# A DLRM tower on one core: products from split halves against fp32 products in row strips, and sixteen looked-up fields against twelve

## What is computed

```python
e = jnp.stack([tbl_0[ids[:, 0]], ..., tbl_38[ids[:, 38]]], axis=1)    # (512, 39, 32), fp32
p, q = e[:, ROW, :], e[:, COL, :]                                     # all 741 pairs i < j
z = jnp.einsum('bpc,apc,bpa->bp', p, w, q)                            # w: (32, 741, 32)
h = jnp.concatenate([z, dense_ctx], axis=1)                           # 741 + 16 = 757
h = jnp.maximum(h @ W_top1 + b_top1, 0.0)                             # 512
h = jnp.maximum(h @ W_top2 + b_top2, 0.0)                             # 256
y = h @ W_top3                                                        # (512, 1)
```

## Time and profile before

| | |
|---|---|
| median of 3 runs | 220.56 us (220.49 to 225.24) |
| span of the profiled execution | 285.0 us |
| PE, DVE, ACT, POOL busy in it | 198.8, 146.6, 97.5, 134.8 us |
| moved by DMA | 31.40 MB |

### The profile page before, as it was taken

One profiled execution on the slowest core, in us unless ns is written; L12 is line 12 of the kernel. 1 busy time (PEld: TensorE's weight loads), 2 busy tenths in 40 slices (PEclk: granted clock), 3 DMA queues, 4 the chain that ended last, 5 costly groups with the idle time before them and its releaser, 6 DMA issues.

```text
span 285.0 us, 2687 instructions
## 1 busy us (share of the span) xinstructions
PE 198.8 (70%) x974; PEld 73.5 (26%) x974; DVE 146.6 (51%) x115; ACT 97.5 (34%) x142; POOL 134.8 (47%) x134
## 2 busy tenths in 40 slices
PE   0048668453212277738798197699899999999996
PEld 0012223000000033213333032243333334344341
DVE  0353794101000027824794266389599779898230
ACT  2516899300000047830540071037127127110032
POOL 7774767777777300776587887200042015007000
PEclk9999797755555559795999669599999999999999
DMA  4869779700000003997266018148715846450000
GB/s 134 257 210 300 285 177 212 164 16 13 14 13 13 9 0 74 300 207 148 50 158 166 12 41 183 41 96 167 167 33 118 183 98 129 98 121 1 0 2 0
DMA packets 11352, 31.40 MB, mean 110 GB/s; under 512 B 3230, under 2 KB 7098, under 8 KB 10379
## 3 DMA queue, kind: packets, MB, share of 16 engines
q1 hardware_dynamic: 7882, 29.45, 42.1%
q0 software_dynamic: 3456, 1.78, 3.5%
HBM read 12.34 MB, written 0.00 MB: 43 GB/s over the span
## 4 chain that ended last, share of the span: by engine, by line
PE 51%; issue 18%; DMA 9%; DVE 7%; SPq 6%; another core or an unknown queue 4%; ACT 3%; DVEq 0%; ACTq 0%
PE t_ps L719 16%; PE z_ps L735 15%; PE z_ps L688 9%; DMA mlp<-tbl 6%; PE side_ps L750 5%; DMA wring<-w_lo 4%; DVE prod L658 3%; SPq L425 2%; PE t_ps L777 2%; DVE prod L629 2%; SPq L431 1%; SPq L475 1%; PE t_ps L765 1%; PE t_ps L770 1%
## 5 line engine op out<-in xcount | busy, mean ns | idle before, releaser
L658 DVE TENSOR_TENSOR prod<-t_ps,eT 128x1536 f32<-128x1536 f32 (+2 forms) x70 | 109.9, 1600 | 79.3 <-PE t_ps L719 49.7
L514 POOL DMA_INDIRECT gathered<-tbl,ids_sb x108 | 104.9, 971 | 53.5 <-issue 31.4
L719 PE MATMUL t_ps<-stack,wring 128*128 128x512 f32 x210 | 72.9, 464 | 12.2 <-issue 6.7
L735 PE MATMUL z_ps<-prod,sel 128*32 128x512 f32 x380 | 57.5, 645 | 4.6 <-issue 4.6
L719 PEld LDWEIGHTS t_ps<-stack,wring 128*128 128x128 f32 x210 | 38.3, 205 | 65.8 <-issue 39.5
L688 PE MATMUL z_ps<-prod,room 125*32 125x512 bf16 x72 | 21.0, 534 | 34.1 <-issue 33.3
L528 POOL TENSOR_TENSOR room<-room,w_hi 128x512 f32<-128x512 f32 x3 | 3.9, 1286 | 66.3 <-ACT w_hi L603 66.3
L629 DVE TENSOR_SCALAR prod<-mlp,slice_rows 125x2048 bf16<-125x2048 f16 x18 | 14.8, 856 | 23.0 <-remote 23.0
L587 ACT ACTIVATE stack<-hi_lo 32x512 fp32r<-32x512 f32 x39 | 24.6, 629 | 2.6 <-issue 1.2
L580 ACT ACTIVATE stack<-eT 32x512 fp32r<-32x512 f32 x39 | 24.4, 625 | 1.0 <-PE t_ps L719 0.7
L750 PE MATMUL side_ps<-room,mlp 128*128 128x512 f32 x32 | 18.4, 660 | 7.7 <-ACT eT L567 7.6
(11 more groups left out here) (49 smaller groups left out, 113.5 us busy)
## 6 DMA issues: line engine op xcount, KB each, us to landing
wring<-w_hi SPq DMA_DIRECT2D x30, 224.0 KB
wring<-w_lo SPq DMA_DIRECT2D x30, 224.0 KB
stack<-stack SPq DMA_DIRECT2D x9, 512.0 KB
w_lo<-wst SPq DMA_DIRECT2D x4, 896.0 KB, 15.2
eT<-hot_ids SPq DMA_DIRECT2D x3, 1024.0 KB
gathered<-tbl,ids_sb POOLq DMA_INDIRECT x108
mlp<-w SPq DMA_DIRECT2D x1, 1536.0 KB
mlp<-tbl SPq DMA_DIRECT2D x12, 125.0 KB
```

What stands on the lines that cost most here:

```text
L514: pool.indirect_dma_start(gathered[:, n % GATHER_BUFS, b, K * r:K * r + K], None, tables[f], bass.IndirectOffsetOnAxis(ap=ids_sb[:, F * b ...
L658: dve.tensor_tensor(prod[:, g % XSLOTS, 0:n, :], t_ps[g % 2][:, 0:n, :], field, ALU.mult).then_inc(multiplied, 1)
L719: mm = pe.matmul(t_ps[g % 2][:, i, :], wring[:, c % WSLOTS, passes % WCHUNK, :].bitcast(F32R), stack[:, J % STACKS, src - G * J, :].bitcas ...
L735: mm = pe.matmul(z_ps[K * (u % G):K * (u % G) + K, :], sel[:, u // G, :], prod[:, g % XSLOTS, t - TILE_BASE[g], :], start=(u < G), stop=(u ...
```

## The change

It rewrites the kernel in these parts:

- **Products.** No halves, no stack, no ring. All weights (55 tiles of 128 columns) are loaded once and used in fp32. A "quad" is block J against block I: its four tiles use the four strips of 32 rows of `eT[:, J, :]` and of the same weight tile, so each product has 32 rows and 128 columns. A block against itself is two products of 64 rows (one of 96 for the last block). DVE multiplies two tiles at a time; three such pairs fit in PSUM, where two groups of three did.
- **Lookups.** Four blocks (0, 1, 2 and 4: 16 fields) instead of three. The upper 16 bits of the table words are used where they lie, as bf16; the two lower bytes become two bf16 parts (two ACT instructions for each block), and the results are put together in `eT` as two 16-bit halves. PE spreads the ids over the partitions itself. The fourth block has ten slices.
- **Gathers.** Six blocks (23 fields, 92 gathers), each with its own buffer. After each gather but the last POOL clears an unused tile of 128 x 256 and waits for the clear before it.
- **Tower.** Early sums in three rounds of 2, 2 and 1 blocks of z; nothing is left of the fifth block for the end.
- All plain loads are issued at the start.

```diff
-HOT_BLOCKS = [0, 1, 3]
-GATHERED = [J for J in range(NBLK) if J not in HOT_BLOCKS]
+LOOKED = [0, 1, 2, 4]
+GATHERED = [J for J in range(NBLK) if J not in LOOKED]
+SMALL = [f for f in range(F) if TABLE_ROWS[f] == 1000] + [f for f in range(F) if TABLE_ROWS[f] == 1250]
+HOT_FIELDS = [SMALL[G * h:G * h + G] for h in range(NHOT)]
+NSLICE = [TABLE_ROWS[fields[0]] // HP for fields in HOT_FIELDS]
...
+for _J in range(NBLK):
+    QUADS += [(_J, _I, FIELDS_IN[_J]) for _I in range(_J)]
+    QUADS.append((_J, _J, 2 if FIELDS_IN[_J] == G else 1))
...
+PAIRS = [(q, i, min(2, QUADS[q][2] - i)) for q in range(NQUAD) for i in range(0, QUADS[q][2], 2)]
+TSLOTS = 3
+XSLOTS = 6
-ROUNDS = [[0], [1], [2], [3]]
+ROUNDS = [[0, 1], [2, 3], [4]]
+KEEP_LEAD = 3
...
+    steps += [("ids", 0), ("lower", 0), ("ids", 1), ("look", 0, 0, 3), ("lower", 1), ("ids", 2), ("look", 0, 3, 8),
+              ("keep", 0), ("lower", 2), ("ids", 3), ("look", 1, 0, 8), ("lower", 3), ("keep", 1), ("look", 2, 0, 8),
+              ("keep", 2), ("quad", 0), ("look", 3, 0, 2), ("quad", 1), ("look", 3, 2, 5), ("quad", 2),
+              ("look", 3, 5, 8), ("quad", 3), ("look", 3, 8, 10), ("keep", 4), ("keep", 3)]
+    sums(1, True)
+    for q in range(4, NQUAD):
+        steps.append(("quad", q))
+        for T in GATHERED[1:]:
+            if q == FIRST_QUAD[T] - KEEP_LEAD:
+                steps.append(("keep", T))
...
-                for i, part in enumerate((w_hi, w_hi, w_lo, w_lo)):
-                    sp.dma_start(wring[K * i:K * i + K, c % WSLOTS, :, :].rearrange("p a b -> p (a b)"),
-                                 part[q:q + K, c // G, :]).then_inc(wring_in[c % WSLOTS], 16)
+            def load_w(J):
+                a, b = W_BASE[J], W_BASE[J + 1]
+                sp.dma_start(w_sb[:, a:b, :].rearrange("p t c -> p (t c)"),
+                             wst[:, P * a:P * b]).then_inc(w_in[J], 16)
...
+                    pool.indirect_dma_start(
+                        gathered[J][:, b, K * r:K * r + K], None, tables[f],
+                        bass.IndirectOffsetOnAxis(ap=ids_sb[:, F * b + f:F * b + f + 1], axis=0),
+                    ).then_inc(rows_in[J], 16)
+                    if pauses:
+                        pool.wait_ge(paused, pauses)
+                    if (J, r, b) != (*fields[-1], NCHUNK - 1):
+                        pool.memset(pause[:, :], 0.0).then_inc(paused, 1)
+                        pauses += 1
...
+                        act.activation(lower[i][h][0:HP, :, :], bytes_of[h][0:HP, :, 1 - i::4], ACT.Copy,
+                                       scale=256.0 if i == 0 else 1.0).then_inc(lower_made, 1)
...
+                        act.activation(words.bitcast(BF16)[:, 1::2], look_ps[h][0], ACT.Copy)
+                        act.activation(words.bitcast(U16)[:, 0::2], look_ps[h][1], ACT.Copy).then_inc(eT_made, 1)
...
+                        dve.tensor_tensor(prod[:, p % XSLOTS, 0:n, :], ps[:, s:s + n, :],
+                                          eT[:, I:I + 1, :].broadcast_to([P, n, B]), ALU.mult).then_inc(multiplied, 1)
...
+                    for r in range(G):
+                        mm = pe.matmul(ids_ps[h][:, r, :], spread[:, G * h + r, :], ids16[:, :], start=True, stop=True)
...
-                            mm = pe.matmul(t_ps[g % 2][:, i, :],
-                                           wring[:, c % WSLOTS, passes % WCHUNK, :].bitcast(F32R),
-                                           stack[:, J % STACKS, src - G * J, :].bitcast(F32R),
-                                           start=(k == 0), stop=(k == len(tile) - 1))
+                        if p >= TSLOTS:
+                            pe.wait_ge(multiplied, p - TSLOTS + 1)
+                        for i in range(first, first + n):
+                            rows = source_rows(q, i)
+                            mm = pe.matmul(ps[:, 2 * (p % TSLOTS) + i - first, :], w_sb[rows, w_tile(q), :],
+                                           eT[rows, J, :], start=True, stop=True)
+                        mm.then_inc(t_made, 1)
```

More of the change, by code:

```diff
@@ L77 @@
+FIRST_TILE = [TILE_BASE[q] + i for q, i, _ in PAIRS]
+PAIRS_THROUGH = [sum(1 for p in PAIRS if p[0] <= q) for q in range(NQUAD)]
+TSLOTS = 3
+XSLOTS = 6
 ZTILES = P // G
 ZM = ZTILES // G
[L81 to L109, removed]
@@ L126, with sources @@
-FIRST_GROUP = [min(g for g in range(NGROUP) if GROUPS[g][0] == J) for J in range(NBLK)]
-ROUNDS = [[0], [1], [2], [3]]
[L128 to L133, removed]
-SEL_LAG = 2
+NZ = -(-NTILE // ZTILES)
+ROUNDS = [[0, 1], [2, 3], [4]]
+SEL_LAG = 2
+KEEP_LEAD = 3
+PACE = 2
+Z_LAG = 2
+PAUSE = 256
+def sources(q):
+    J, I, n = QUADS[q]
+    if I < J:
+        return [[(r, c) for c in range(G)] for r in range(n)]
+    if FIELDS_IN[J] == G:
+        return DIAGONAL
+    return [LAST_DIAGONAL]
@@ L137, in plan @@
+_free = [z_row(t, c) for t in range(NTILE) for c in range(G) if (t, c) not in _taken]
+DENSE_ROWS = []
+while len(DENSE_ROWS) < NDENSE // 2:
+    _a, _b = _free[:2]
+    if _a // P == _b // P:
+        DENSE_ROWS.append((min(_a, _b), abs(_a - _b)))
+    _free = _free[2 if _a // P == _b // P else 1:]
+DENSE_BLOCKS = sorted({first // P for first, _ in DENSE_ROWS})
 def plan():
     steps, done = [], 0
[L155 removed]
@@ L156, in plan @@
[L156 to L161, removed]
+    early = [(m, n) for n in range(len(ROUNDS)) for m in range(M1)]
+    since = 0
     def sums(upto, exact):
@@ L205, in plan, with there @@
-    sums(NGROUP - 2, True)
-    steps += [("early", *e) for e in early]
-    steps += [("long", k) for k in range(long, NZ - 1)]
-    late = [("late", m, zb) for m in range(M1 - 1) for zb in range(EARLY_Z, NZ - 1)]
-    steps += late[:-1]
-    sums(NGROUP - 1, True)
-    steps += late[-1:]
-    return [step for step in steps if step not in POOL_WORK.values()]
+    def there(zb):
+        names = [s[:2] for s in steps]
+        return ("z", zb) in names and sum(s[0] == "quad" for s in names[names.index(("z", zb)):]) > Z_LAG
@@ new lines, in plan @@
+    steps += [("ids", 0), ("lower", 0), ("ids", 1), ("look", 0, 0, 3), ("lower", 1), ("ids", 2), ("look", 0, 3, 8),
[4 more added lines that the diff above has]
+    for q in range(4, NQUAD):
+        J = QUADS[q][0]
+        steps.append(("quad", q))
+        since += 1
+        for T in GATHERED[1:]:
+            if q == FIRST_QUAD[T] - KEEP_LEAD:
+                steps.append(("keep", T))
+        near = any(0 < FIRST_QUAD[T] - KEEP_LEAD - q <= 1 for T in GATHERED)
+        if early and since >= PACE and not near and all(there(zb) for zb in ROUNDS[early[0][1]]):
+            steps.append(("early", *early.pop(0)))
+            since = 0
+        sums(q - SEL_LAG, False)
+        sums(q - SEL_LAG - 1, True)
@@ L215 @@
+    sums(NQUAD - 2, True)
+    steps += [("early", *e) for e in early]
+    sums(NQUAD - 1, True)
+    return steps
 PLAN = plan()
-LAST_FIRST = [M1 - 1] + list(range(M1 - 1))
-assert NGROUP % 2 == 0
-SPLITS = [s[1:] for s in PLAN if s[0] == "split"]
 TURNS = [s[1] for s in PLAN if s[0] == "keep"]
-assert all([s[1] for s in PLAN if s[0] == part] == TURNS for part in ("halve", "stack"))
+SUMS = [s for s in PLAN if s[0] == "sums"]
+EARLY = [s[1:] for s in PLAN if s[0] == "early"]
+SUMS_THROUGH = [next(i + 1 for i, s in enumerate(SUMS) if s[1] + s[2] >= FIRST_TILE[p] + PAIRS[p][2])
+                for p in range(NPAIR)]
```

672 lines of the change are left out of this document (261 added, 411 removed).

## The result

The changed kernel takes **221.62 us** as the median of 20 runs (216.78 to 225.10), the kernel before 222.30 in 20 runs on the same chip (220.49 to 225.24). The ratio of the fast runs alone (those within 1.5% of a kernel's fastest, 5 and 19 of the 20) is 0.984 [0.980, 0.989]: 1.6% faster, no change by the 2% bound. The forecast was 199 us, 184 to 226, with 0.75 on faster. The time lies within the range, but not in my own case (190 to 207).

What follows compares the result with a forecast made beforehand. PE was taken to bound the pair products, with DVE close behind. Start 47, pair products 132, waiting 2 and end 16.5 gave 197.5; half the method's earlier shortfall of 4 to 5 made it 199 us, range 184 to 226.

Steps and rivals of the forecast that it cites:

- my own case: Whole kernel: 190 to 207 us, with the pair stage 125 to 137 and a start up to 5 us later; chance 0.58.
- The start: Lookups mixed with quads 0 to 3, before the pair products: that stage begins at 47 us instead of 50.
- POOL's list: Rival: gathers on POOL bound the kernel, 5 + 80 p + 74 us, 195 at p = 1.45, 227 at 1.85; chance 0.20.
- The pair products: Stage after the lookups: 119 us of PE work and 109 of DVE, taken as 132 us with some smoothing.
- The quad of fp32 strips: PE in the pair stage: four fp32 products on different row strips take 1.05 us, between 0.99 and 3.44.
- the smoothing: Pair stage: three slots even out PE and DVE, giving 132 us between 136 quad by quad and 122 perfectly smoothed.
- The gathers: POOL, with clears between: one gather per 1.45 us, block 8 there at 121, 2 us of waiting counted.
- The end: From the last sum through the second layer to the end of the span: 16.5 us instead of 21.
- A reason of mine: Kernel before, 47 to 103 us: back-to-back gathers not blamed for PE's slow stretch, as they also ran before 23 us.
- the slower rival: Pair stage: strips of rows don't run beside one another; 230 us if only pairs overlap, 287 if none; chance 0.16.
- The gather of 1.41 us: Kernel before: some gathers took 1.41 us instead of 0.94 while DVE compared, taken as support for POOL bounding.
- Theory P: Experiments' theory: POOL's clears slow DVE's compares and so the lookups; without clears 3 to 6 us faster overall.

Runs made afterwards that it cites:

- late quads: The changed kernel with quads 0 to 3 moved behind the ten slices of the fourth lookup: 253.34 us, against 263.93 for the changed kernel in that group.

## Why the prediction was wrong, step by step

**The start failed, by 19 us.** The step read: "Blocks 0 to 2 are done by 32 us ... Then come ten slices (7 to 8 us) mixed with quads 0 to 3 (about 4), and the turns of blocks 4 and 3 (2). The stage of pair products begins at 47 us". I added PE's own times for the mixed stretch, as if what PE waits for there were ready. The blocks were done at 29.3, better than forecast; quad 4 came at 65.9. Of the list's order I had read PE's part and not DVE's, where each round's compares stand behind multiplies that wait for PE. 10.3 us are PE's waits for compares, and most of the rest is the low clock that came with them. The same PE list with DVE's compares ahead starts quad 4 at 48.70, close to the 47. That 221.6 us lies inside the range at all is owed to the room I had left for POOL's list, not for this.

**The pair products: mechanism right, size 5 us short.** From 65.9 to the last multiply's end at 203.1, where my term for the end begins, they took 137.2 us against 132. The quad of fp32 strips, the term that I called the unknown, was 1.07 us for 1.05. By the Trainium skill ("TensorE: Matmul & The Clock Gate", measured speedup) it would be an estimated 1.12; the trace lies between the two. What was off is the smoothing: the quad-by-quad sum had 136, and I took 4 off for three slots. That sum itself counts 42 quads for blocks 2 to 8 where the plan has 41, so it should have been 134. A two-block early part is 1.92 us where I had 1.72, worth 2 with the one-block parts, and two early parts waited 0.7 us each for ACT. With these the sum without smoothing comes to the 137 measured: the three slots smoothed next to nothing.

**The gathers: right in kind.** 1.51 us apart instead of 1.45, done at 141, and no wait where I had 2 us. **The end** was 16.4 (203.1 to 219.5) for 16.5. The device time is 1.7 above the span, which the sum left out. All together, from the sum of 197.5: + 19 + 5 - 2 + 1.7 = 221.2, the time of the profiled execution.

**A reason of mine fell that didn't enter the sum.** Of the 56 us in which PE of the kernel before stood nearly still, I wrote that POOL "issued them back to back before 23 us as well, so I don't blame them". The experiments speak against that: in the changed kernel the same picture comes with gathers back to back and goes when they are spaced or left out. The kernel before wasn't run with other gathers, so for it this is an inference. My reason was weak as well: before 23 us PE of that kernel had 5.07 us of work. In the kernel without clears, too, PE ran undisturbed until 18.9 us, though gathers ran back to back from 3.0 on. (The 56 products of the stretch are also more than the four slices that I counted.) Cutting the stretch out was right for the runs that were shown, but on the other chips every run of the kernel before takes 286 to 296 us, which I put down to such a stretch, and the change is worth 10% there.

**The rivals.** The strips overlap, so the slower rival is out. POOL's list doesn't bound at 1.51 us; the rival's formula, 5 + 80p + 74, gives 200 there (and 215, not 216, at 1.7). It began to count once the start was mended: with late quads and 320 columns (1.56 us apart) it gives 204 where 213.5 were measured. It named the wrong block: PE waits at the turns of blocks 6 and 7 (until 81.67 and 105.70), not at block 8's. The gather of 1.41 us that I took as its sign ran beside an addition of two tensors on DVE (30.45 to 31.68) as much as beside a compare (31.59 to 32.34). Neither rival was what happened.

## What to carry to other kernels

In a list that several engines walk through, follow each mixed stretch as a chain across the engines before adding up times: ask of each instruction what stands ahead of it in its own queue, and whether that waits for the engine it is to feed. Work that makes operands for another engine belongs ahead of work that consumes that engine's results. And where POOL gathers, look in the profile for PE's idle time under "issue". Where it stands there, a slightly longer gap between the gathers can be worth more than a better order (here 35 us against 10.6 with 256 columns), and is tried with one number.

## What the runs showed of the hardware

- On some chips PE's instructions nearly stop while POOL issues gathers 1.25 us apart (one recorded product in 2.80 us); with a 256-column clear between them (1.53 us apart) it still loses 13.7 us to "issue" in 85, with a 320-column clear none (on another chip, see the caution above). The chip of the 20 runs lost nothing at 1.51. What ties PE to the gathers isn't shown; leaving the gathers out cures it (221.74 us for 263.93), though plain transfers of the same size run.
- The clears slow DVE's compares: one takes 0.756 us in the mean with none, 0.887 with 256 columns and 0.995 with 512, all in the changed kernel's order. The 256 columns cost 4 to 5 us over 34 compares, so Theory P holds as a small part of DVE's time; that it reaches the end of the kernel isn't shown. The Trainium skill's "GPSIMD Engine Reference", key points, says that POOL shares its SBUF interfaces with DVE and that they contend when DVE runs in a two-port mode or reads two inputs from SBUF. These numbers agree in that POOL's clears slow DVE's compares; in which mode a compare runs, no run shows.
- The granted clock drops where PE is made to wait, and the drop goes with the waits: from 30 to 66 us, on one chip and without gathers, it is 0.69 with 10.5 us of waits for compares and 1.00 with the quads late, where there are none.
